# Graph attention in two layers: second-layer weights held in SBUF, a four-tile x ring, and four orders of work rewritten

## The reference, cut to what matters

```python
# layer 0
q, k, v = x @ Wq.T + bq, x @ Wk.T + bk, x @ Wv.T + bv
a = q @ k.T / sqrt(512) + adj + adj
x1 = layernorm(x + softmax(a) @ v)
# layer 1, 8 heads of 64
feats = einsum('nf,hfd->hnd', x1, W)
dense = leaky_relu(e_self[:, :, None] + e_neigh[:, None, :])
dense = dense + (-1e10 * (1.0 - adj))
out = layernorm(x1 + relu(softmax(dense) @ feats + b))
```

## Time and profile before

| | us |
|---|---|
| median of 3 runs | 1775.04 |
| lowest and highest | 1771.71, 2446.5 |
| the profiled execution, its own time | 1778.22 |
| its span, first to last instruction | 1776.3 |
| mean granted TensorE clock | 0.957 |

### The profile page before, as it was taken

One profiled execution on the slowest core, in us unless ns is written; L12 is line 12 of the kernel. 1 busy time (PEld: TensorE's weight loads), 2 busy tenths in 40 slices (PEclk: granted clock), 3 DMA queues, 4 the chain that ended last, 5 costly groups with the idle time before them and its releaser, 6 DMA issues.

```text
span 1776.3 us, 36165 instructions
## 1 busy us (share of the span) xinstructions
PE 1600.0 (90%) x13172; PEld 1283.5 (72%) x13172; DVE 1352.9 (76%) x2241; ACT 621.6 (35%) x1085; POOL 1245.2 (70%) x1461
## 2 busy tenths in 40 slices
PE   7798979999999999999999999999999999997820
PEld 3333468888888888888887878788888787875600
DVE  5544437887988888888797888788888888877646
ACT  4343402333333333333332333333333333333427
POOL 3323304988887888788887888888888888886533
PEclk9899989999999999999999999999999999998955
DMA  6434278888888888888888888888888888881668
GB/s 240 151 112 146 107 243 290 265 263 271 260 282 259 287 255 294 263 290 255 280 257 265 262 282 262 276 260 282 263 291 259 284 258 276 252 266 57 200 209 292
DMA packets 281859, 438.13 MB, mean 247 GB/s; under 512 B 26960, under 2 KB 127312, under 8 KB 281680
## 3 DMA queue, kind: packets, MB, share of 16 engines
q1 hardware_dynamic: 276560, 419.01, 73.3%
q0 software_dynamic: 5120, 16.78, 2.9%
HBM read 390.60 MB, written 45.09 MB: 245 GB/s over the span
## 4 chain that ended last, share of the span: by engine, by line
PE 64%; DVE 11%; POOL 8%; DMA 7%; issue 5%; ACT 4%; SPq 1%; ACTq 0%; DVEq 0%; POOLq 0%
PE S L607 32%; PE O L684 26%; DMA xring<-w_scratch 5%; PE X L735 3%; DVE big L963 2%; POOL big L589 1%; POOL pfc L556 1%; POOL pc L570 1%; DMA vsum<-vsum_scratch 1%; PE X L724 1%; DVE pfc L1079 1%; POOL pfc L557 1%; POOL pfc L525 1%; DVE cand L1052 1%; DVE big L1101 1%
## 5 line engine op out<-in xcount | busy, mean ns | idle before, releaser
L607 PE MATMUL S<-yb,xring 128*128 128x256 f16 x6144 | 710.2, 273 | 11.4 <-DMA xring<-x_scratch 11.4
L607 PEld LDWEIGHTS S<-yb,xring 128*128 128x128 f16 x6144 | 602.5, 98 | 84.9 <-issue 11.9
L684 PE MATMUL O<-big,pc 128*128 128x256 f16 (+1 forms) x4608 | 599.8, 276 | 11.8 <-DMA vsum<-vsum_scratch 5.8
L808 ACT ACTIVATE pc<-pfc 128x128 f16<-128x128 f32 (+1 forms) x512 | 289.1, 574 | 862.1 <-PE O L684 549.0
L684 PEld LDWEIGHTS O<-big,pc 128*128 128x128 f16 x4608 | 453.2, 99 | 80.8 <-issue 7.8
L570 POOL TENSOR_TENSOR pc<-pfc,pc 128x768 f16<-128x768 f32 x240 | 396.0, 1650 | 137.1 <-ACT pc L808 136.1
L1101 DVE TENSOR_TENSOR big<-S,big 128x512 f32<-128x512 f32 x256 | 175.6, 686 | 177.5 <-PE S L607 177.0
L556 POOL TENSOR_TENSOR pfc<-pfc 128x256 f32<-128x256 f32 x256 | 233.1, 911 | 79.8 <-ACT pfc L901 79.1
L1113 DVE TENSOR_TENSOR mx<-mx,big 128x512 f32<-128x512 f32 x240 | 238.6, 994 | 8.2
L565 POOL TENSOR_TENSOR sacc<-sacc,pfc 128x256 f32<-128x256 f32 x240 | 212.6, 886 | 0.0
L1079 DVE TENSOR_TENSOR pfc<-pfc 128x256 f32<-128x256 f32 x256 | 186.4, 728 | 0.1
(11 more groups left out here) (130 smaller groups left out, 1190.8 us busy)
## 6 DMA issues: line engine op xcount, KB each, us to landing
xring<-x_scratch SPq DMA_DIRECT2D x512, 256.0 KB, 3.9
big<-in_adjT SPq DMA_DIRECT2D x256, 256.0 KB, 4.2
piece<-in_adj SPq DMA_DIRECT2D x256, 256.0 KB, 3.9
vsum<-vsum_scratch SPq DMA_DIRECT2D x256, 128.0 KB, 3.3
xring<-w_scratch SPq DMA_DIRECT2D x128, 256.0 KB, 3.9
big<-in_xT SPq DMA_DIRECT2D x8, 1024.0 KB, 8.3
yb<-y_scratch SPq DMA_DIRECT2D x16, 512.0 KB, 4.8
hc<-in_x SPq DMA_DIRECT2D x32, 256.0 KB, 4.7
```

Of the source, the lines that this page charges most:

```text
L607: mm = pe.matmul(psum, sta(a, k), mov(b, k), start=(k + a + b == 0), stop=(k == n - 1 and a == 1))
L684: mm = pe.matmul(dst, pc[:, e % 2, a, sta * P:(sta + 1) * P], mov, start=start, stop=(k == NP - 1 and a == 1 and closes))
L808: return nc.scalar.activation(dst, src, ACT.Copy, scale=scale)
```

## The change

- `w1p` gets an SBUF tensor of its own (16 KB a partition) and is read by `feats` directly; the scratch copy and the 128 weight loads through `xring` go.
- To make room: `xring` has 4 tiles for 5, `piece` 2 for 3, the half-logit ring 20 slots for 21, and `load_adj` runs 2 chunks ahead for 3. `bvb` moves to `mx`.
- `feats` is cut in four parts of three matmuls, one in each of four steps (offsets 4 to 7 and 9 to 12); the second transpose moves to offset 8, and the evictions to 7 and 12. In the last block all stays close together, with a bank of its own for each product.
- Setup: VectorE does `x_lo` of the next group between the second and the third `value_rows`, not after the queries of the group; two queries, not one, go ahead of the second `value_hi` and `value_lo`.
- SyncE asks for the first adj chunks and the first four x tiles at the start of the last group; the wait for all value parts moves from before the scores to before the first `values`.
- ScalarE's loop does the exponential of chunk `s-17` before the high parts of `s-18`.
- `load_x1` reads a block (512 KB) a step, from the third step of the last block's values.

```diff
-    AHEAD = 3
-    SLOTS = LAG + 2
-    NX = 5
+    AHEAD = 2
+    SLOTS = LAG + 1
+    NX = 4
-    NSC = 3
+    NSC = 2
+        w1p = sb("w1p", [P, KC, 2, D], F16)
...
+        def transposes_at(s, j):
+            b = block_at(s, 3 + 5 * j)
+            last = block_at(s, 3 + 2 * j)
+            return last if last == NB - 1 else b if b is not None and b < NB - 1 else None
+
+        def feats_at(s, j):
+            parts = [(block_at(s, 4 + 5 * j + kc), kc) for kc in range(KC)]
+            last = block_at(s, 4 + 2 * j)
+            if last == NB - 1:
+                return [(last, kc) for kc in range(KC)]
+            return [(b, kc) for b, kc in parts if b is not None and b < NB - 1]
+
+        def evict_at(s, j):
+            b = block_at(s, 7 + 5 * j)
+            last = block_at(s, 7 + j)
+            return last if last == NB - 1 else b if b is not None and b < NB - 1 else None
+
+        def x1_bank(t):
+            return S[0][:, :] if t == NT - JB else X[:, :]
+
+        def feats_bank(t):
+            return X[:, :] if t < NT - JB else O[t % JB][:, :]
...
             for g in range(NG):
+                if g == NG - 1:
+                    for c in range(AHEAD):
+                        load_adj(c)
+                    for k in range(2):
+                        sp.wait_ge(x_out[k], 16 * (NG // 2))
+                    sp.wait_ge(yp_ready, (NG - 1) * KC)
+                    for i in range(NX):
+                        load_passing(i)
...
-            def load_x1(e):
-                first, last = 2 * e * EG, min(2 * (e + 1) * EG, NT - JB)
+            def load_x1(b):
+                first, last = b * JB, (b + 1) * JB
...
             def values(e):
                 b, k = divmod(e, NP)
+                if e == 0:
+                    pe.wait_ge(v_lo, NP)
...
-                else:
+                elif t < NT - JB:
                     pe.wait_ge(f_set, t)
...
+            def feats(t, kc):
+                if kc == 0:
+                    pe.wait_ge(x1T_set, t + 1)
+                    if t == 0:
+                        pe.wait_ge(w1_lo, 1)
+                    if t >= NT - JB:
+                        pe.wait_ge(c_added, 8 * NB)
+                for a, m in ((0, 0), (0, 1), (1, 0)):
+                    mm = pe.matmul(feats_bank(t), x1T[:, a, kc, :], w1p[:, kc, m, :], start=(kc + a + m == 0),
+                                   stop=(kc == KC - 1 and a == 1))
+                mm.then_inc(f_part, 1)
...
                 value_hi(2 * g)
-                query_hi(g, 0)
+                for jc in range(2):
+                    query_hi(g, jc)
                 value_hi(2 * g + 1)
-                for jc in range(1, KC):
+                for jc in range(2, KC):
                     query_hi(g, jc)
...
+                e = s - LAG + 2
+                if 0 <= e < NC:
+                    act.wait_ge(sub_done, e + 1)
+                    if e >= 2:
+                        act.wait_ge(lo_first, e - 1)
+                        act.wait_ge(lo_rest, e - 1)
+                        act.wait_ge(sum_done, e - 1)
+                    nc.scalar.activation(pfc[:, e % 2, 0:512], ring[:, e % SLOTS, :], ACT.Exp, scale=-2.0
+                                         ).then_inc(exp_done, 1)
                 e = s - LAG + 1
...
             for g in range(NG):
-                for i in range(GT):
+                for i in range(2):
+                    value_rows(g * GT + i)
+                if 1 <= g < NG - 1:
+                    x_lo(g + 1)
+                for i in range(2, GT):
                     value_rows(g * GT + i)
                 value_lo(2 * g)
-                query_lo(g, 0)
+                for jc in range(2):
+                    query_lo(g, jc)
                 value_lo(2 * g + 1)
-                for jc in range(1, KC):
+                for jc in range(2, KC):
                     query_lo(g, jc)
-                if g + 2 < NG:
-                    x_lo(g + 2)
```

More of the change, by code:

```diff
@@ L154, in adj_resnorm_kernel @@
         vf = ring[:, 16:20, :].rearrange("p (b k) n -> p b k n", b=2)
-        bvb = ring[:, 20, :]
+        bvb = mx[:, :]
         x16 = [xring[:, 0:4, :].rearrange("p i (a c n) -> p i a c n", a=2, c=KC),
@@ L215, in adj_resnorm_kernel @@
             sem, ("usum_ready", "thr_set", "ok_chain", "count_ready", "flag_set"))
-        x1r_in = [sem(f"x1r_in{e}") for e in range(NE // 2)]
+        x1r_in = [sem(f"x1r_in{e}") for e in range(NB // 4)]
         got_in = [sem(f"got_in{e}") for e in range(NE)]
@@ L265, in turn @@
             return NP * (b + 1) + LAG
-        LAST = turn(NB - 1) + 8
+        LAST = turn(NB - 1) + 14
         def block_at(s, offset):
@@ L295, in passing @@
                     yield s, ("x", c, 1)
[L296 to L300, removed]
         stream = list(passing())
@@ L386, in load_adj @@
                              ).then_inc(adj_in[c % 4], 16)
+            store_x(0)
+            for g in range(NG):
+                if g == NG - 1:
[6 more added lines that the diff above has]
+                        load_passing(i)
+                if g + 2 < NG:
+                    load_x(g + 2)
+                if g + 1 < NG:
+                    store_x(g + 1)
+                for t in range(2 * g, 2 * g + 2):
+                    sp.wait_ge(v_lo, t + 1)
+                    sp.dma_start(vs_d[t], vsum[:, t % NVS].rearrange("p a n -> p (a n)")).then_inc(vs_out[t % NVS], 16)
+                sp.wait_ge(y_lo, (g + 1) * KC)
+                ys = yb[:, :, :, :, :] if g < NG - 1 else y_last
+                sp.dma_start(y_d[2 * g:2 * g + 2].rearrange("b p n -> p b n"), ys.rearrange("p b a c n -> p b (a c n)")
+                             ).then_inc(y_out, 16)
+                if g == NG - 2:
+                    sp.wait_ge(y_out, 16 * (NG - 1))
+                    for b in range(2):
+                        sp.dma_start(yb[:, b].rearrange("p a c n -> p (a c n)"), y_d[b]).then_inc(y_in[b], 16)
             def load_vsum(e):
@@ L418, in _ @@
             sp.wait_ge(u_set, 2)
-            sp.wait_ge(w1_out, 16)
             n_passed = 0
@@ L747, in _ @@
                 for j in range(JB):
-                    b = block_at(s, 3 + 2 * j)
+                    b = transposes_at(s, j)
                     if b is not None:
                         transpose_x1(b * JB + j)
-                    b = block_at(s, 4 + 2 * j)
-                    if b is not None:
-                        feats(b * JB + j)
+                    for b, kc in feats_at(s, j):
+                        feats(b * JB + j, kc)
                 if 0 <= s - LAG < NC:
```

93 lines of the change are left out of this document (19 added, 74 removed).

## The result

The changed kernel takes 1754.24 us (median of 4 runs, 1751.9 to 1755.8); the kernel before took 1774.63 beside it. The ratio is 0.989, with an interval of 0.987 to 0.991: 20 us less, where I had forecast 49, and outside my range of 1700 to 1750. By the prediction's own line of 2% this is no change, to which I had given 0.23. One of the four executions of the kernel before took 2446.5 us and is left out of the ratio. The profiled execution has a span of 1754.0 against 1776.3.

A forecast was written before the change was run, and what follows sets the result against it. The prediction took TensorE to set the main loop's pace, VectorE and GpSimd having 16 to 18% to spare. Its terms, -31.8 - 4.7 - 19.3 + 8.0 - 1.2 = -49.0 us, took 1775.0 to 1726 us, range 1700 to 1750.

The forecast's parts named there:

- Setup: Projections: with x_lo moved, seven groups take 20.7 us each, one wait behind group 1 stays; net -31.8 us.
- First scores: Start of scores: early x requests remove the 11.42 us wait, a late fifth tile and four-tile ring cost some; -4.7 us.
- The ring of four: x tiles in the first 19 steps: four tiles, not five, make about half come late; +3 us, between 0 and 45.
- Main loop: Second-layer waits go, late low parts behind a block's turn cost some back; net -19.3 us.
- I charge 0.8 us in each of 15 blocks: +12: Main loop behind a turn: low parts have zero slack, then -0.3 us a step on; +12 us, from 0 to 39.
- The 31.3: Main loop: 20.4 us of weight waits and 10.9 of second-transpose waits for the eviction go.
- The lock: Last block: two-SBUF-input VectorE and GpSimd instructions exclude each other; without GpSimd, loop 3.6 us and net 0; 4.1 kept.
- Last block: Its values: ScalarE's order lengthens the chain to 4.1 us a chunk, +16.8, less 8.8; net +8.0, from -9 to +17.
- the end: After the values: last transpose no longer waits for the eviction, no 1.5 MB read beside the last stores; -1.2 us.
- the 8.8: Last block: smaller x1 reads end waits for sums of values (4.50, 1.3 us) and 3 us at lower clock; -8.8 us.
- rival 1: Main loop: VectorE and GpSimd have no spare time behind a turn; 2.1 us lost a block, 1745 us; chance 0.17.
- Rival 3: Main loop: SyncE's queue starves the four x tiles, four steps a block lose 1.3 us, 78 us, 1804; chance 0.05.

The follow-up runs named there:

- d: The changed kernel with ScalarE's copies ahead of the exponential again, for the last block's chunks only; 1738.7 us (ratio 0.982).
- c: The kernel before with only the setup's new orders (x_lo between second and third value rows, two queries ahead of the second value parts); 1743.4 us (ratio 0.982).
- g: The changed kernel with ScalarE's copies first, and the first x tiles and adjacency pieces asked for after the last group's stores; 1704.5 us (ratio 0.962).
- a: The changed kernel with ScalarE's copies (high parts) of s-18 before the exponential of s-17 again; 1700.3 us (ratio 0.957).
- l: The changed kernel with VectorE's difference cut to 2 x 8 columns from 2 x 128, from the third chunk on; 1730.7 us (ratio 0.975).
- i: The changed kernel with GpSimd's running sum of the exponentials cut to 8 columns from 256; 1729.1 us (ratio 0.974).
- b: The kernel before with only ScalarE's new order, the exponential of s-17 before the high parts of s-18; 1817.3 us (ratio 1.022).
- f: The changed kernel with ScalarE's copies first, and x1 read back in four large requests, not fifteen of 512 KB; 1699.8 us (ratio 0.960).

## Why the prediction was wrong

- **Setup (-31.8, measured -26.4).** The mechanism was right: groups of 20.7 us, and the one large wait behind group 1 (3.46 late with the row behind it at 8.11; 6.2 together, put at 5.1). Of the miss of 5.4 us, 2.5 lie in the head, which I took over unchanged: the row that starts at 42.71 in the earlier trace rows starts at 45.25, mostly because 24 matmuls behind the first wait took 7.04 us, where before they took 5.35. I also left out a wait of 1.17 in group 4. The head differs between executions of the same setup code too: eight kernels with it ended their projections between 194.7 and 198.3. Between after (198.3) and `d` (194.9) the difference is that the matmuls behind the first two waits took 7.04 and 8.11 us in after, at a mean granted clock of 0.76 and 0.65, and 5.35 and 6.67 in `d`, at 1.00 and 0.79. Alone, in `c`, these edits brought 30; its profiled execution had one of the faster heads (195.4).
- **First scores (-4.7, measured -3.8).** The late fifth tile was right (4.44 where I had 3.8). The ring of four behind it waited 2.2 us in after, 0.2 in `d` and 3.85 in `g`, for my 3. I left out what the 4.44 brings with it: the 96 matmuls behind it took 13.4 us at a mean granted clock of 0.79, where 96 take 11.1 at 2.78 for 24.
- **Main loop (-19.3, measured +3.3 with the first block).** The step that failed is "I charge 0.8 us in each of 15 blocks: +12". The 31.3 that I took off is about right, as the 33.3 of `a` show. But the order costs (1251.4 - 1216.0) + (76.5 - 75.3) = 36.6 us, 2.4 a block: three times my charge, near my upper bound of 39. Two things were wrong in it. I worked with 0.87 us for the difference. Behind a turn it starts under GpSimd's low part, in 55 steps of after, and takes up to 1.86. And I asked in how many steps the way is longer than TensorE's, when I should have asked what closes on itself. With the exponential first, ScalarE can't make the copies of a chunk before VectorE has subtracted the next, VectorE can't before its difference is out, and that stands behind GpSimd's low part, which needed the copies of the chunk before. It takes 4.40 us for a step of TensorE's 4.91, so a late step is made good by only 0.5 us in the next. That each extra piece on VectorE or GpSimd (an eviction of 0.68, a gather of 1.27) makes it late again is read from the rows, not tested. In the old order the copies don't wait for the subtract. `l` and `i` each shorten one instruction and each get about 20 us back in the fourteen blocks; how much is the ring's and how much GpSimd's own work, which stands still for only 0.20 us in the 4.40, isn't separated.
- **The lock.** The Trainium skill, SBUF - State Buffer (SBUF: two separate sides), says that a VectorE instruction with two SBUF inputs and a GpSimd instruction that reads SBUF exclude each other for a whole instruction. I weighed this against the last block and set it aside, as a chance of a better result. The trace agrees: 16 columns under GpSimd took 1.61 us, and GpSimd in turn waits for a VectorE instruction of this kind that was at work first (last section). It was the loop where it mattered, and it made the time longer.
- **Last block (+8.0, and -1.2 for the end; measured +4.6).** The chain of 4.06 was 4.1 in the forecast. The order's price is 170.65 - 155.5 = 15.1 (I had 16.8; in the old kernel `b` shows 9.0), the rest brought 166.1 - 155.5 = 10.6 (I had 8.8 + 1.2). But I gave the 8.8 to the size of the x1 reads, and `f` shows no gain from their size by itself.
- **Rivals.** What happened is rival 1, "the chain takes the loop's gain", with 2.4 us a block where it asked for 2.1, and 5 us less in the setup. I gave it 0.17. My argument against it, that the values almost never waited for low parts before, spoke of the order that the change removes. My sign of it, waits for low parts of over 2 us a block, would have missed it: they are 1.65, since part of the loss stands in busy time. Rival 3 (the ring of four starved) did not occur: 3.0 us of waits for x tiles in the loop of `a`, where it had asked for 78.

## What to carry to other kernels

When a change reorders the work of an engine in a software pipeline, look for a ring through several engines that the new order closes, and add up its whole length by the longest durations that its rows take beside the others, not by the median. Where that comes near the bounding engine's step (here 4.40 of 4.91 us), a delay is made good only slowly, and the price isn't that of the two steps that one works out by hand (here 2.4 us a block, not 0.8). And take a change of many parts apart: one line order here cost 54 us, more than twice what all of it together brought.

## What the runs showed of the hardware

- A VectorE instruction with two SBUF inputs that starts under a GpSimd `tensor_tensor` ends 0.03 us (16 columns), 0.28 (256 columns) or 0.55 us (512 columns, the maximum) behind GpSimd's end, on the median. Alone they take 0.17, 0.41 and 0.69. So it stands, and then does its own work.
- It works the other way too, by who is at work first. GpSimd's sum of 256 columns (L565) takes 0.72 to 0.74 us alone, and 1.17 where VectorE's maximum is still at work when it starts (in `l`, one timeline):

```profile
746.16 1.44 DVE L1130 TENSOR_TENSOR mx<-mx,big 128x512 f32<-128x512 f32 x1
747.01 1.17 POOL L565 TENSOR_TENSOR pfc<-pfc 128x256 f32<-128x256 f32 x1
747.52 0.69 DVE L1096 TENSOR_TENSOR pfc<-pfc 128x16 f32<-128x16 f32 x1
```

The difference that starts under it isn't the cause: in 13 rows of `l` and 16 of after no difference starts under the sum, and it takes 1.17 to 1.18 all the same; in 18 rows of `l` the maximum only starts under it, and it takes 0.72.
- One setup code ended its projections up to 3.6 us apart in eight executions (194.7 to 198.3). Between the slowest, after, and `d` the difference lay almost all in the matmuls behind the first two waits.
